# An audio tower on one core: where 16 weight pieces are prepared, when ranks are counted, when the second matrix is loaded

## The reference, cut to what matters

```python
h = tok(x)                                  # 3 frames spliced, 192 -> 128
h = h + recurrence(norm(h))                 # 256 complex states, h = h * lam + B u
h = h + first_mixture(norm(h))              # 16 experts, top 2, 128 -> 512 -> 128
h = h + sparse_attention(norm(h))           # 8 heads; 25 queries chosen by sampled scores
h = h + second_mixture(norm(h))             # 64 experts, 42 chosen, 128 -> 256 -> 128

# first_mixture: silu(x w1[e]) is summed over the tokens of each expert, divided by
# their count, multiplied once by w2[e]; tokens get a weighted sum of two such rows.
# sparse_attention: M = max - mean of q . k over 38 sampled keys; the 25 queries of
# largest M attend to all keys, the other positions get the mean value.
```

## Time and profile before

| | |
|---|---|
| median of 3 runs | 2063.67 us (2062.18 to 2066.14) |
| the profiled execution | 2067.39 us, span 2065.7 us |
| busy: PE, DVE, ACT, POOL | 91%, 81%, 67%, 70% of the span |
| mean granted TensorE clock | 0.939 |

### The profile page before, as it was taken

One profiled execution on the slowest core, in us unless ns is written; L12 is line 12 of the kernel. 1 busy time (PEld: TensorE's weight loads), 2 busy tenths in 40 slices (PEclk: granted clock), 3 DMA queues, 4 the chain that ended last, 5 costly groups with the idle time before them and its releaser, 6 DMA issues.

```text
span 2065.7 us, 50535 instructions
## 1 busy us (share of the span) xinstructions
PE 1870.1 (91%) x17038; PEld 1349.7 (65%) x17038; DVE 1676.4 (81%) x4833; ACT 1378.0 (67%) x2149; POOL 1455.0 (70%) x1098
## 2 busy tenths in 40 slices
PE   7887436789989978999999999999999999999998
PEld 5555213456669855777777777777777777777776
DVE  5887736555678788899999999999999999999998
ACT  4134525424435545888888888888888888888886
POOL 2216679559800032888888888888888888888887
PEclk9998768789989965999999999999999999999999
DMA  3011289523200010000000200000100000000000
GB/s 93 21 35 63 81 246 257 124 67 94 90 1 1 22 63 1 2 2 0 0 0 3 82 2 0 0 0 35 49 1 0 0 0 2 2 10 11 10 11 19
DMA packets 64334, 77.56 MB, mean 38 GB/s; under 512 B 38932, under 2 KB 47028, under 8 KB 62132
## 3 DMA queue, kind: packets, MB, share of 16 engines
q1 hardware_dynamic: 61364, 70.08, 11.7%
q0 software_dynamic: 2816, 5.45, 0.8%
HBM read 42.97 MB, written 24.08 MB: 32 GB/s over the span
## 4 chain that ended last, share of the span: by engine, by line
PE 58%; DVE 3%; issue 2%; ACT 1%; POOL 0%; ACTq 0%; DVEq 0%; POOLq 0%
PE bank L2679 30%; PE bank L2662 28%; DVE m_work L2553 1%; DVE m_best L2550 1%; DVE m_work L2544 0%; PE bank L2632 0%; DVE m_ut L1269 0%; ACT m_h L2485 0%; DVE m_best L2543 0%; DVE m_ex L2555 0%; DVE h L2591 0%; DVE m_red L2556 0%; DVE m_row L2536 0%; POOL m_diag L1255 0%; ACT m_hidden L2482 0%
## 5 line engine op out<-in xcount | busy, mean ns | idle before, releaser
L2679 PEld LDWEIGHTS bank<-weights,m_h 128*128 128x128 f16 x10752 | 649.6, 98 | 194.4 <-DVE hc L2582 82.6
L2430 POOL TENSOR_TENSOR m_h<-m_hidden,m_h 128x896 f16<-128x896 f32 x384 | 725.9, 1890 | 32.0
L2679 PE MATMUL bank<-weights,m_h 128*128 128x128 f16 x10752 | 724.6, 219 | 10.7 <-POOL m_h L2430 2.1
L2582 DVE SCALAR_TENSOR_TENSOR hc<-bank,m_shares,hc 128x128 f32<-128x128 f32 x2688 | 727.2, 342 | 4.3 <-PE bank L2679 4.3
L2482 ACT ACTIVATE m_hidden<-bank,m_b 128x896 f32<-128x896 f32 x384 | 386.9, 1007 | 197.6 <-PE bank L2662 197.5
L2567 DVE TENSOR_TENSOR m_h<-bank,m_h 128x896 f16<-128x896 f32 x384 | 419.2, 1092 | 116.8 <-ACT m_h L2485 116.7
L2428 POOL TENSOR_SCALAR m_h<-m_hidden 128x896 f16<-128x896 f32 x384 | 360.8, 939 | 117.9 <-ACT m_hidden L2482 99.5
L2662 PE MATMUL bank<-m_u_first,weights 128*128 128x448 f16 (+1 forms) x1536 | 417.8, 354 | 5.5 <-DVE h L2591 5.5
L2662 PE MATMUL bank<-m_u_second,weights 128*128 128x448 f16 (+1 forms) x1536 | 417.7, 354 | 0.0
L2479 ACT ACTIVATE bank<-bank,m_b 128x896 f32<-128x896 f32 x384 | 377.6, 983 | 0.6 <-PE bank L2662 0.6
L2485 ACT ACTIVATE m_h<-bank 128x896 f16<-128x896 f32 x384 | 349.1, 909 | 0.0
(11 more groups left out here) (359 smaller groups left out, 2153.9 us busy)
## 6 DMA issues: line engine op xcount, KB each, us to landing
weights<-expert_factors SPq DMA_DIRECT2D x12, 1024.0 KB, 8.8
lru_w_in<-e_w_dram SPq DMA_DIRECT2D x16, 512.0 KB, 4.5
expert_factors<-lru_w_out SPq DMA_DIRECT2D x16, 512.0 KB, 4.3
ew_raw<-e_w_dram SPq DMA_DIRECT2D x16, 512.0 KB, 3.9
weights<-w_dram SPq DMA_DIRECT2D x16, 256.0 KB, 2.8
weights<-w_dram SPq DMA_DIRECT2D x4, 1024.0 KB, 6.6
expert_factors<-ew_made SPq DMA_DIRECT2D x8, 512.0 KB, 3.0
xs<-x_dram SPq DMA_DIRECT2D x4, 996.0 KB, 11.8
```

The lines of the kernel that those rows point to most:

```text
L2430: g.tensor_tensor(h1[:, x, 1], hidden[:, x], h1[:, x, 0], ALU.subtract).then_inc(second_of[1], 1)
L2582: last = v.scalar_tensor_tensor(acc[:, m * TW:(m + 1) * TW], y[q][:, (n - start) * TW:(n - start + 1) * TW], shares[:, m, e:e + 1], acc[:, ...
L2679: last = t.matmul(y[q][:, (n - start) * TW:(n - start + 1) * TW], factors[:, m, n * TW:(n + 1) * TW], k.weights[:, grp % 2, 2 + m, at], st ...
```

## The change

**Late pieces.** Pieces 16 to 31 leave the first mixture. They are cut into 32 halves of 512 columns, which are loaded, made and stored in the sampling block, two for each chunk. ACT makes the first part and a copy scaled by 1/64 (`act_piece`), DVE the second part (`dve_piece`). The scaled copy has one buffer: ACT waits for the `split` of the half before. ACT's halves stand behind its copies of q = 1 and q = 3, DVE's behind the subtractions of q = 1 and q = 3.

**POOL's pieces.** The three pieces ahead of the first diagonal go; the loop makes piece c - 1 behind diagonal c, for c = 1 to 15, and piece 15 behind the loop. In SP's list, load n + 1 stands at the end of round n, behind the stores of both halves of round n. The wait for the last stores moves into the block of `attend`.

**Second matrix.** The four quarters of w2 are loaded as soon as the 16 outputs are made and w1 is split, ahead of the blank rows, into four places.

**First mixture.** SP's list there has transposes alone. Every sixth set is summed by ACT, in two halves of 384 columns with an accumulated sum; DVE skips it. Buffers move.

**Recurrence.** `pe_rank` stands ahead of output 3 and not of output 2, and the second half of `state_part` ahead of `dve_place`.

```diff
@@ -966,8 +966,9 @@
                 if p >= 2:
                     sp.wait_ge(w_wide, p - 1)
                 sp.dma_start(wst[:, p % 2, :], a["w1"][:, p * piece:(p + 1) * piece]).then_inc(raw_in[p % 2], 16)
+            mixture.sync_second(sp, y_ready)
             routing.sync_fill(sp)
-            mixture.sync(sp, y_ready)
+            mixture.sync(sp)
 
         @block.gpsimd
         def _(pool):
...
-            mixture.pool(pool)
 
...
@@ -1115,12 +1115,12 @@
                     if g == 0:
                         normed(2 * PERG + 2 * i)
                         normed(2 * PERG + 2 * i + 1)
+                if g + 1 < NGR:
+                    state_part(g + 1, 1)
                 if g:
                     routing.dve_place(dve, g - 1)
                     routing.dve_rows(dve, g - 1)
                     routing.dve_weights(dve, g - 1)
-                if g + 1 < NGR:
-                    state_part(g + 1, 1)
                 for i in range(2, STEP):
                     add(g, i)
                     split(STEP * g + i)
...
@@ -1218,7 +1218,7 @@
                     spread_rstd(2 * PERG)
                     spread_rstd(2 * PERG + 1)
                 for i in range(STEP):
-                    if i == 2 and g:
+                    if i == STEP - 1 and g:
                         routing.pe_rank(pe, g - 1)
...
+    BY_ACT = 6
+
+    def act_sums(self, n):
+        return n % self.BY_ACT == self.BY_ACT - 1
+
+    def dve_sets(self, n):
+        return n - n // self.BY_ACT
+
+    def wait_summed(self, eng, n):
+        if self.act_sums(n):
+            eng.wait_ge(self.silu, n + 1)
+        else:
+            eng.wait_ge(self.summed, self.dve_sets(n + 1))
 
...
+        quarter = E0 * FC * 128 // 4
+        flat_ut = ut.rearrange("p g i c -> p (g i c)")
+        homes = (k.weights[:, 1].bitcast(F32).rearrange("p a b -> p (a b)")[:, 0:quarter], w_in.rearrange("p a b c d -> p (a b c d)"),
+                 w_out.rearrange("p a b c d -> p (a b c d)")[:, 0:quarter], flat_ut[:, self.RING * ST:self.RING * ST + quarter])
+        self.xt = flat_ut[:, 0:self.RING * ST].bitcast(F16).rearrange("p (n m t) -> p n m t", n=self.RING, m=2)
+        self.w2 = [home.rearrange("p (e f d) -> p e f d", e=E0 // 4, f=FC) for home in homes]
...
-        sp.dma_start(self.w2[:, es], self.k.a["w2"][:, es]).then_inc(self.k.w2_in, 16)
-
-    def sync(self, sp, outputs_made):
-        k, routing, late = self.k, self.routing, self.late
+        sp.dma_start(self.w2[q], self.k.a["w2"][:, es]).then_inc(self.k.w2_in, 16)
+
+    def sync_second(self, sp, outputs_made):
         sp.wait_ge(outputs_made, NC)
-        late.sync_load(sp, 0)
-        late.sync_load(sp, 1)
-        sp.wait_ge(k.w0_split, NC)
-        self.sync_down(sp, 0)
+        sp.wait_ge(self.k.w0_split, NC)
+        for q in range(4):
+            self.sync_down(sp, q)
+
+    def sync(self, sp):
+        k, routing = self.k, self.routing
...
             sp.dma_start_transpose(self.xt[:, j % self.RING], k.slots[bass.ds(rows[j], ST), :]).then_inc(self.x_in[j % self.RING], 16)
-            if j in self.W2_AT:
-                self.sync_down(sp, 1 + self.W2_AT.index(j))
-            if j >= self.KEEP_FROM and (j - self.KEEP_FROM) % self.KEEP_EVERY in (0, 2):
-                late.sync_keep(sp)
-        while late.kept < late.count:
-            late.sync_keep(sp)
-        late.sync_kept(sp)
 
...
             act.wait_ge(self.up, j + 1)
-            self.nc.scalar.activation(self.set_banks(j), self.set_banks(j), ACT.Silu).then_inc(self.silu, 1)
+            if self.act_sums(j):
+                for f in range(self.FP):
+                    at = j % self.PARTS * self.FP + f
+                    last = self.nc.scalar.activation(self.set_banks(j)[:, f], self.set_banks(j)[:, f], ACT.Silu,
+                                                     accum_out=self.part[:, j // self.PARTS, at:at + 1])
+            else:
+                last = self.nc.scalar.activation(self.set_banks(j), self.set_banks(j), ACT.Silu)
+            last.then_inc(self.silu, 1)
 
...
         for j in range(PARTS * NST):
+            if self.act_sums(j):
+                continue
             dve.wait_ge(self.silu, j + 1)
             v.tensor_reduce(self.part[:, j // PARTS, j % PARTS * FP:(j % PARTS + 1) * FP], self.set_banks(j), X, ALU.add).then_inc(self.summed, 1)
...
+            k.late_weights = LateWeights(nc, k, first)
             norm = Normed(nc, k, first, "at")
-            stats = Statistics(nc, k, first, "n3", CH, HALF, NC, NC // 2)
+            squares = k.late_weights.room[:, 0:DEEP * CH].rearrange("p (n c) -> p n c", n=DEEP)
+            stats = Statistics(nc, k, first, "n3", CH, HALF, NC, NC // 2, squares)
             ut = norm.ut
...
-                k.expert_weights.sync_pieces(sp, *PIECES_N3)
-                k.expert_weights.sync_pieces(sp, *PIECES_SAMPLE)
+                k.expert_weights.sync_load(sp, 0)
+                k.expert_weights.sync_load(sp, 1)
+                sp.wait_ge(stats.var, NC + DEEP)
+                k.late_weights.sync_load(sp, 0)
+                k.late_weights.sync_load(sp, 1)
+                for n in range(2 * GROUP):
+                    for s in range(2):
+                        k.late_weights.sync_load(sp, 2 * n + 2 + s)
+                        k.late_weights.sync_keep(sp, 2 * n + s)
+                    if n:
+                        k.expert_weights.sync_keep(sp, n - 1)
+                    if 1 <= n < 2 * GROUP - 1:
+                        k.expert_weights.sync_load(sp, n + 1)
+                k.late_weights.sync_kept(sp)
+                k.expert_weights.sync_keep(sp, 2 * GROUP - 1)
 
             @block.gpsimd
             def _(pool):
@@ -1599,12 +1625,11 @@
                 nc.clear_and_free_semaphores(spent)
                 g.iota(line[:], [[HALF, 2]], base=0, channel_multiplier=1,
                        allow_small_or_imprecise_dtypes=True).then_inc(made, 1)
-                k.expert_weights.pool_pieces(pool, *PIECES_N3)
-                first, end = PIECES_SAMPLE
                 for c in range(NC):
                     norm.pool_diagonal(pool, c, c % 2, stats)
-                    if 1 <= c <= end - first:
-                        k.expert_weights.pool_pieces(pool, first + c - 1, first + c)
+                    if c:
+                        k.expert_weights.pool_pieces(pool, c - 1, c)
+                k.expert_weights.pool_pieces(pool, NC - 1, NC)
...
                                                  kx[:, j, q])):
                             last = nc.scalar.activation(dst, k.bank[0:HALF, 4 + q % 2, m * 128:(m + 1) * 128], ACT.Copy)
                         last.then_inc(kx_copied, 1)
+                        if q % 2:
+                            k.late_weights.act_piece(act, c, q // 2)
 
...
                         dve.wait_ge(peaked, m + 1)
                         v.tensor_tensor(m_all[:, q % 2, bass.ds((2 * c + q // 2) * NH, NH)], peak[:, q % 2],
                                         sc[:, :, NS:NS + 1].rearrange("p a b -> p (a b)"), ALU.subtract).then_inc(measured, 1)
+                        if q % 2:
+                            k.late_weights.dve_piece(dve, c, q // 2)
                         if isinstance(c, int) and TAKE <= c <= TAKE + NU // 8 and q == 1:
                             choice.dve_round(dve, c - TAKE == NU // 8)
...
+        @block.sync
+        def _(sp):
+            k.expert_weights.sync_kept(sp)
+
         @block.scalar
...
+HALF_PIECE = PIECE // 2
+PIECES_POOL, PIECES_LATE = (0, 2 * GROUP), (2 * GROUP, NG * GROUP)
...
+        self.room = sb("room", [128, 5 * HALF_PIECE])
+        self.raw = self.room[:, 0:2 * HALF_PIECE].rearrange("p (j n) -> p j n", j=2)
+        self.wide = self.room[:, 2 * HALF_PIECE:3 * HALF_PIECE]
+        self.made = self.room[:, 3 * HALF_PIECE:].bitcast(F16).rearrange("p (j q n) -> p j q n", j=2, q=2)
...
     def sync_load(self, sp, i):
         if i >= self.count:
             return
-        n = self.first + i
+        n = self.first + i // 2
         src = self.k.a["e_w1"] if n % GROUP < PIECES else self.k.a["e_w2"]
         if i >= 2:
             sp.wait_ge(self.raw_read, i - 1)
-        first = n // GROUP * GE * HC * 128 + n % PIECES * PIECE
-        sp.dma_start(self.raw[:, i % 2, :], src[:, first:first + PIECE]).then_inc(self.raw_in[i % 2], 16)
-
-    def sync_keep(self, sp):
-
-        i = self.kept
-        if i >= self.count:
-            return
-        n = self.first + i
-        mat, cols = n % GROUP // PIECES, slice(n % PIECES * PIECE, (n % PIECES + 1) * PIECE)
-        self.sync_load(sp, i + 2)
+        first = n // GROUP * GE * HC * 128 + n % PIECES * PIECE + i % 2 * HALF_PIECE
+        sp.dma_start(self.raw[:, i % 2, :], src[:, first:first + HALF_PIECE]).then_inc(self.raw_in[i % 2], 16)
+
+    def sync_keep(self, sp, i):
+        n = self.first + i // 2
+        start = n % PIECES * PIECE + i % 2 * HALF_PIECE
```

(18 more changed lines are left out.)

60 lines of the change are left out of this document (14 added, 46 removed).

## The result

The changed kernel takes 2299.2 us (median of 4 runs, 2293.9 to 2300.6) against 2063.3 us before: a ratio of 1.114 (95% interval 1.112 to 1.116), 11% slower. The forecast was 2283, in a range of 2235 to 2333.

| stage | before | after | difference |
|---|---|---|---|
| start to the first matmul of the first mixture | 283.3 | 287.5 | +4.2 |
| first mixture's loop, to the last reduction | 114.4 | 84.4 | -30.0 |
| from there to the first spread of sampling | 58.3 | 49.1 | -9.2 |
| first spread to the first query copy of the attention block | 128.0 | 408.2 | +280.2 |
| from there to the second mixture's first product | 246.5 | 247.0 | +0.5 |

A forecast was written before the change was run, and what follows sets the result against it. POOL's pieces through SP's list were taken to bound the first mixture, PE sampling, with POOL just keeping up; -41 + 4 - 7 + 226 + 24 + 13 = +219 us gave 2283 us, range 2235 to 2333.

The forecast's parts named there:

- The two rings: Sampling: wait chains through ACT's scaled copy (14.9 us a chunk) and SP's load of POOL's piece (23.5); the longer decides, +226 us.
- parts of 11.7 and 11.8 us: Long sampling ring: 11.7 us from spread to split (c, 1), then 11.8 for issue, landing 3.9, POOL's piece and diagonal.
- Which chunks: Sampling: long ring closed in chunks 2 to 13, twelve of them; chunks 0, 1 and 14 have the short ring.
- The clock: Sampling: PE restarts at half clock after each wait, adding 2.6 of 4.4 us to the ring; granted clock near 0.7.
- Short chunks and end: Sampling: chunks 0, 1 and 14 at 15.3 us, +24 us; POOL's late piece 15 and tail at the end, +13 us.
- First mixture: First mixture's loop: paced by POOL's pieces through SP's list; without them it takes 73 us, -41 us (bounds -48 to -25).
- ACT is the limit: First mixture's loop: ACT needs 70 us for its sets, at 1.2 us per summed set, plus 3 us: 73 us.
- Rank: Recurrence: rank matmuls behind output 2 make group 3's place, rows and sends late, +4.4 us (3 to 5).
- Start of sampling: Start of sampling: PE's 4.96 us wait for the first diagonal goes and its clock improves, -7 us (-5 to -9).
- Only the short ring: Rival for sampling: POOL has its pieces in time, fifteen chunks of 15.3 us, 2147 us; chance 0.05.
- Neither ring closes: Rival for sampling: ACT and DVE run their halves in holes without holding PE, -44 us, 2020 us; chance 0.06.
- The break-even: Sampling: up to 10.2 us a chunk the change costs nothing, 2.9 us a chunk against a gain of 44.

The follow-up runs named there:

- e1: Changed kernel with SyncE's load of GpSimd's next piece moved ahead of the late halves of the round: 2224.1 us, ratio 1.0755.
- e2: Changed kernel with ScalarE scaling each late half in place instead of into the single buffer; SyncE's load waits for the split instead: 2256.1 us, 1.0943.
- e7: Changed kernel with VectorE's late halves made one chunk earlier, SyncE's list left as changed: 2163.1 us, ratio 1.0478.
- e4: Changed kernel with 24 unused matmuls on TensorE ahead of each spread from chunk 1 on, after one more subtraction wait: 2279.4 us, 1.1037.
- e8: e5 with rank matmuls again ahead of output 2, every tenth instead of sixth set on ScalarE, expert numbers loaded 32 at a time: 2061.0 us, 0.9963.
- e9: e8 with SyncE's store of GpSimd's piece n - 1 and load of piece n + 2 between the two halves of round n: 2041.7 us, 0.9898.
- e12: e9 with the store of GpSimd's piece n - 1 back at the head of round n, the load left between the halves: 2037.6 us, 0.9873.
- e5: Changed kernel with the edits of e1 and e2, VectorE's halves one chunk earlier, and GpSimd's piece stored ahead of the halves: 2066.3 us, 0.9996.
- e11: Kernel before the change with only the rank matmuls moved behind output 2 and the second state_part ahead of the places: 2069.9 us, 1.0028.
- e10: e9 with VectorE computing 8 of 512 columns of each late half, the rest left zero: 2028.6 us, 0.9826.

## Why the prediction was right, step by step

The rings, the order that closes them and the waits that show them were as forecast. The total is closer than its parts: sampling came 17 us and the first mixture 11 us over their terms, and 13 us less in a stage that the forecast left alone made up for half of it. That part is luck.

**The two rings.** The mechanism was as forecast: parts of 11.7 and 11.8 us at full clock, 23.5 together, and 2.6 for the clock. Measured are 15.2 and 12.3 us, intervals of 27.26, so +239 us where +226 stood. The second part was right but for the landing: 4.5 us (median from 475 to 830 us) for 3.9. (The 3.9 of the earlier trace rows has loads ahead of sampling in it, with little beside them; from 457 to 585 us the old kernel's median is 4.3.) The first is all that the clock touches: 11.7 + 2.6 = 14.3 forecast, 16.1 with all of the clock, 15.2 measured. e1 opens the one ring, and e2 takes the single buffer out of it; e7, where the split comes early, leaves the ring through SyncE alone.

**Which chunks.** I put the long intervals at chunks 2 to 13 and the short ones at 0, 1 and 14. The trace has them long from chunk 1 on (448.33 to 472.40) to chunk 12: piece 2, needed in `work(2)`, is already loaded behind split (1, 1), as the prediction's own sentence on piece c + 1 says for c = 1. The count of twelve held, the places were one off, and it cost nothing.

**The clock.** Granted 0.62 in the stretch where I said near 0.7; e4 prices it at 2.1 us an interval at least, where 2.6 stood: its matmuls fill only the wait ahead of the spread.

**Short chunks and end.** +24 and +13 forecast, 280.2 - 239 = +41 measured; chunk 0 took 15.45 us (432.88 to 448.33) for 15.3, and TensorE waits 12.9 us at the end of sampling for GpSimd's tail, whose last select ends at 828.87, ahead of the next block's start at 829.20.

**First mixture.** -41 forecast, -30.0 measured, inside the bounds but for a reason that I had not seen. TensorE's timeline of the loop after, all runs of matmuls:

```profile
287.54 21.61 PE L1413 MATMUL bank<-lru_ut,weights 128*128 128x384 f16 x104 [35.00 <-DMA lru_ut<-expert_slots]
309.30 4.48 PE L1413 MATMUL bank<-lru_ut,weights 128*128 128x384 f16 x24
319.35 8.10 PE L1413 MATMUL bank<-lru_ut,weights 128*128 128x384 f16 x32 [5.57 <-issue]
327.70 3.31 PE L1413 MATMUL bank<-lru_ut,weights 128*128 128x384 f16 x16 [0.25 <-DVE lru_xc L1384]
331.16 9.28 PE L1413 MATMUL bank<-lru_ut,weights 128*128 128x384 f16 x48
340.59 6.10 PE L1413 MATMUL bank<-lru_ut,weights 128*128 128x384 f16 x32
350.89 19.03 PE L1413 MATMUL bank<-lru_ut,weights 128*128 128x384 f16 x88 [4.21 <-issue]
```

The holes of 5.57 and 4.21 us are the same as the two of before (5.58 at 330.81 and 4.35). I had read the one in the earlier trace rows as a hole of the transposes. Its releaser says "issue", and the line behind it (L71, `load_rows`) is that of the expert numbers, which TensorE's own sequencer (PEldq) loads for 16 tiles at a time:

```profile
L71 PEldq FUSED_REGOPS  x43: 146/146/165, 256.0 to 350.4; - x43
L71 PEldq TENSOR_LOAD <-ro_owner_i x3: 1151/1313/1337, 254.6 to 346.1; - x3
```

In the first hole after, one load of 1.15 us starts at 313.4, and the 16 numbers are clamped one behind the other from 314.6 to 319.1, 0.29 us apart; TensorE goes on at 319.35. Before, the same work stands from 324.7 to 330.5, ahead of 330.81. Transposes that come sooner cannot shorten it. The step that failed is "ACT is the limit. With 3 us to fill and empty the ring": ScalarE stood another 15.0 us for TensorE inside the loop: 10.9 in the two waits at the holes (6.12 and 4.82), 2.4 in short ones right behind them, where TensorE's granted clock is low (0.75 from 320 to 330 us, 0.72 from 350 to 360), the rest in waits of 0.2 to 0.5. 66.5 + 15.0 + 3 = 84.5, with 84.4 measured. The other size of this term was off the other way: a set summed by ScalarE took 0.96 us (293.37 to 294.33), where 1.2 stood, so ScalarE was busy 66.5 us and not 70. ScalarE's timeline at one such set:

```profile
293.37 0.50 ACT L1372 ACTIVATE bank<-bank 128x384 f32<-128x384 f32 x1
293.74 0.22 ACT L1372 ACTIVATION_READ_ACCUMULATOR bank<-bank 128x1 f32 x1
293.83 0.51 ACT L1372 ACTIVATE bank<-bank 128x384 f32<-128x384 f32 x1
...
294.24 0.22 ACT L1372 ACTIVATION_READ_ACCUMULATOR bank<-bank 128x1 f32 x1
294.33 3.78 ACT L1375 ACTIVATE bank<-bank 128x768 f32<-128x768 f32 x5
```

With 32 numbers at a time one hole is left (4.2 us in e8), and the loop, there with every tenth set on ScalarE, took 79.6, 80.2 and 78.2 us in e8, e9 and e12.

**Rank.** +4.4 forecast, +4.2 to the first matmul; undone in e8 (285.0 against 289.0 in e5), alone in e11 (+4.8 us in the whole). Right, within a scatter of 3 us: the first matmul starts between 287.2 and 290.6 in the nine profiles with this part, between 281.8 and 285.0 in the four that undo it.

**Start of sampling.** -7 forecast (-5 to -9), -9.2 measured.

**Outside the forecast.** The second mixture is 13.3 us shorter in the changed kernel, and in the twelve profiles that carry the change or most of it (the changed kernel, e1 to e10 and e12) it takes 1219.6 to 1223.0 us, while e11 has 1235.7. Its instructions are the same and the clock is full in both. A window of 400 us in the middle, before and after:

```profile
940.00:1340.00 400.00, 397.25 (x4534) 289.45 (x4533) 364.69 (x1009) 337.85 (x379) 355.96 (x252) 1.00 0.03 11
```

```profile
1185.00:1585.00 400.00, 400.00 (x4590) 290.17 (x4588) 369.59 (x1022) 342.34 (x383) 360.04 (x256) 1.00 0.03 11
```

TensorE has 2.75 us of holes in the one and none in the other, and does 4590 products for 4534. The cause is not the rank's part: e11 has it and is slow there, e8 has it undone and is fast. What else it is stays open; no run separates the other parts. Without it the kernel would stand at 2312 us, within the range too.

**The rivals.** "Only the short ring" (2147) is what e1 was to show; it gave 2224, because an interval with that ring, once every chunk has it, takes 19.2 us and not 15.3 (the lower clock and VectorE's stretched splits stand in it; no run prices them apart), and because the store of GpSimd's piece closes another ring in the last four, 25 us each. "Neither ring closes" (2020) was not reached: with the third and the fourth wait opened as well, which I had not named, and with the mixture's edits, e9 and e12 stand at 2042 and 2038. The break-even that the rival gave, 10.2 us a chunk, fits e5 (10.1 us, ratio 0.9996), in part by luck: the first mixture gained 11 us less than its 44 us assume, and the second mixture 13 that they don't have.
